# Two attention blocks: packing the output rows and softmax sums of all heads densely by on-chip transfers, with one normalisation and one output projection per batch element

## The chip, the cores and the metric

The kernel runs on one core of a Trainium2 chip. The metric is the device time of one execution, in microseconds. Five engines run their own instruction streams and meet at semaphores: PE (TensorE, matrix products), DVE (VectorE), ACT (ScalarE), POOL (GpSimd) and SP (SyncE), which here issues nearly all transfers. A wait is an instruction in the stream of the engine that waits, so everything behind it on that engine waits too.

## The reference, cut to what matters

The program is a two-layer transformer: attention, mixture of experts, attention again, and two local-attention layers. Only the two attention blocks are touched. For each of 8 batch elements (512 tokens, 128 channels, 16 heads of 8 channels) both compute

```
scores = q[h] @ k[h].T * scale          # 512 x 512 per head
out[h] = softmax(scores) @ v[h]         # 512 x 8 per head
y = concat(out over 16 heads) @ Wo + bo # 128 x 128 projection
x = x + gate * y
```

Block 0 is causal and shares one key/value head among its query heads; block 1 is not causal and has 16 key/value heads.

## The kernel before, in words

`attend` (L608) is called once per block. A batch element is cut into 4 **units** of 4 heads. A unit has 16 **tiles** (`k`, `h`): 128 of the 512 keys for one head. Loops run batch element, unit `q`, `k`, `h`; the first and the last batch element are written out, the 6 between them are a hardware loop. So a block has 8 x 4 = 32 units.

Each unit goes through the scores twice. The first scores (`a_tile`, L703, run two units ahead) give the row maxima (`maxima`, DVE, L920). `split_max` (POOL, L858) splits them into three bf16 parts, `turn_max` (PE, L721) transposes them, `copy_rows` (ACT, L830) copies them to `mrows`, and `move_max` (SP, L667) moves them with 4 small on-chip transfers into rows 72 to 74 of the query tile `Q`, one per head. The second scores (`b_tile`, L733) therefore come out with the maximum already subtracted. Their first tile in a unit waits for these 4 transfers (`m_loaded`). `exp` (ACT, L821) turns each into `probs`; block 0 then masks future keys on POOL (`mask_future`, L875). `pv` (L744) multiplies 4 heads' `probs` with `V`; one head takes 32 partitions of the bank `OB`: 8 with output rows, one with the softmax sum (a column of ones in `vpad`, L196), 23 with zeros.

Normalising a unit, one unit later: `copy_out` (ACT, L835) copies `OB` to `osum`; `turn_sums` (PE, L760, 4 transposes) turns it; `invert_sums` (DVE, L930) inverts the 16 columns of sums; `repeat_inverses` (POOL, L884) repeats each 32 times; `spread_inverses` (PE, L770, 4 transposes) turns that back; `normalise` (DVE, L937) multiplies; `out_project` (PE, L778) adds the unit's part of the projection in bank `YB`, with a `wo` that is padded with zeros. After 4 units `output` (DVE), `residual` (POOL) and `store` (SP) finish the batch element.

The order is written out by hand. PE takes in each tile step first `a_tile`, then `b_tile`. In step (1,3) come `turn_max` and `pv`, `out_project` is at (1,1), `turn_sums` at (2,1), `spread_inverses` at (3,1), and the last `pv` of a unit is at (0,3) of the next. SP's order in a unit is the following: wait until the unit before has ended its last `pv` (L683), 13 loads for the unit three ahead (`load`, L648: 9 to `Q`, 3 to `K`, 1 to `V`), then `move_max` for the next unit, and in unit 2 also one store and one load. The banks are 3 for first scores, 2 for second scores, and `OB`, `MB`, `YB`.

Of the kernel before, what the change touches and what calls it, by code (L numbers as in the profile page):

```python
# [11 lines left out]
ALU = mybir.AluOpType  # L12
# [3 lines left out]
P = 128  # L16
# [3 lines left out]
UNITS = 4  # L20
# [126 lines left out]
def setup_projection(g):  # L147
# [35 lines left out]
    with nc.Block() as block:  # L183
# [7 lines left out]
        def _(pool):  # L191
# [4 lines left out]
            pool.memset(g.vpad[:, :, :, D:D + 1], 1.0)  # L196
# [367 lines left out]
def setup_attention(g):  # L564
# [4 lines left out]
    g.wo = g.sb("wo", [P, 2, UNITS, C])  # L569
# [6 lines left out]
    g.zero = g.sb("zero", [P, CH * UH * VW])  # L576
    g.seen = g.sb("seen", [P, 1])
    g.osum = g.sb("osum", [P, N])
    g.rsum = g.sb("rsum", [P, CH, UH])
    g.rspread = g.sb("rspread", [P, CH, UH, VW])  # L580
# [6 lines left out]
        "m_loaded", "b_scores", "exp", "masked", "pv", "o_copied", "sums", "rsum", "rspread", "spread", "onorm", "yacc",  # L587
# [4 lines left out]
    with nc.Block() as block:  # L592
        @block.sync
        def _(sp):
            sp.dma_start(g.wo[:, :, :, :], g.ins["wo"]).then_inc(g.as_["setup"], 16)
            sp.dma_start(g.bo[:, :], g.ins["bo"]).then_inc(g.as_["setup"], 16)
            sp.wait_ge(g.as_["setup"], 32 * n_setup)
# [10 lines left out]
def attend(g, layer, x, x_out):  # L608
# [36 lines left out]
    with nc.Block() as block:  # L645
        @block.sync
        def _(sp):
# [25 lines left out]

            def store(i):
# [22 lines left out]
            batches(sp, batch)  # L697
            store(hi)
# [3 lines left out]
        def _(pe):  # L702
# [18 lines left out]
            def turn_max(i, u):  # L721
# [3 lines left out]
                if u >= 2:  # L725
                    pe.wait_ge(s["onorm"], i * 4 + u - 2)
# [6 lines left out]
            def b_tile(i, q, k, h):  # L733

                n = q * per + k * UH + h
                t0 = first_query(k)
# [23 lines left out]
            def turn_sums(i, q, m):  # L760

                pe.wait_ge(s["o_copied"], i * 4 + q + 1)
                pe.wait_ge(s["onorm"], i * 4 + q)
                if m is not None:
                    pe.wait_ge(s["mrows"], i * 4 + m + 1)
                for k in range(CH):
                    mm = pe.transpose(MB[:, k * P:(k + 1) * P], g.osum[:, k * P:(k + 1) * P], g.ident[:, :])
                mm.then_inc(s["sums"], 1)

            def spread_inverses(i, q):  # L770

                pe.wait_ge(s["rspread"], i * 4 + q + 1)
# [1446 lines left out]
```

## Time and profile before

| | us |
|---|---|
| median of 3 runs | 2834.71 (2826.03 to 2836.15) |
| the profiled execution's own time | 2839.19 |
| its span | 2837.5 |
| busy PE / DVE / ACT / POOL | 2243.7 / 1628.8 / 1321.0 / 1076.5 |
| granted PE clock, mean | 0.881 of 2.4 GHz |

"Busy" is the time in which an engine has an instruction under way; matmuls overlap, so the busy time of PE is more than its work. The second scores run from 206 to 1623 us, with the expert stage between the two blocks. Times in the rows are microseconds from the start of the span, unless marked ns. SPq is SP's own queue of instructions: the time of such a row is the time that issuing took, not that of the transfer.

### The profile page before, as it was taken

Reading aid. Unit: us, or ns where it says so; the run is one execution under the profiler, and the core shown is the slowest. Engines: PE = TensorE matmul, PEld = TensorE weight load, DVE = VectorE, ACT = ScalarE, POOL = GpSimd, SP = SyncE. Lnnn points to the kernel's source line nnn. Section 1 sums busy time; section 2 is a strip of 40 time slices with the busy share of each in tenths; the row PEclk is TensorE's granted clock in tenths of the full one; section 3 lists DMA queues with packets and bytes.
Section 4 is the critical chain, followed back from the end, with each engine's and each line's share of the span. In section 5 each row is a group of like instructions: output and inputs, shape, how many; then the busy total and the mean of one; then the engine's idle time right before and its main releaser. Section 6 shows DMA issues by size and latency. Waiting matters only on the chain. (4 is left out here: it accounts for less than half of the span.)

```text
span 2837.5 us, 47372 instructions
## 1 busy us (share of the span) xinstructions
PE 2243.7 (79%) x13156; PEld 1254.2 (44%) x13156; DVE 1628.8 (57%) x3408; ACT 1321.0 (47%) x3058; POOL 1076.5 (38%) x1306
## 2 busy tenths in 40 slices
PE   4649999955381663899999866999999999999996
PEld 2324444434261442233333243555555555555553
DVE  3436666624012332777777436777777677777772
ACT  0115566620130111466666604666666666666662
POOL 2314444422305232011111124655655655555550
PEclk9759999975695665799999958999999999999997
DMA  3322222110223223222222121000000000000000
GB/s 96 123 91 57 69 62 67 55 69 18 73 86 105 69 83 91 67 70 68 65 65 73 31 90 43 9 11 11 15 11 11 12 16 16 22 15 15 15 12 11
DMA packets 114411, 140.99 MB, mean 50 GB/s; under 512 B 15888, under 2 KB 77075, under 8 KB 114064
## 3 DMA queue, kind: packets, MB, share of 16 engines
q1 hardware_dynamic: 112272, 135.74, 16.0%
q0 software_dynamic: 2048, 4.16, 0.5%
q8 instruction: 42, 0.69, 0.1%
q14 instruction: 49, 0.40, 0.0%
HBM read 89.81 MB, written 49.28 MB: 49 GB/s over the span
## 5 line engine op out<-in xcount | busy, mean ns | idle before, releaser
L927 DVE TENSOR_REDUCE M_sb<-bank 128x1 f32<-128x512 f32 (+3 forms) x1024 | 557.2, 583 | 304.7 <-PE bank L718 162.9
L827 ACT ACTIVATE probs_sb<-bank 128x512 f32<-128x512 f32 (+3 forms) x1024 | 487.6, 514 | 306.2 <-PE bank L741 301.3
L1780 ACT ACTIVATE l_p_sb<-bank,l_nb_sb,l_inv_sb 128x192 f32<-128x192 f32 x512 | 257.2, 506 | 369.7 <-DVE l_nb_sb L1964 368.2
L715 PE MATMUL bank<-K_sb,Q_sb 72*128 72x512 bf16 (+3 forms) x1024 | 360.6, 358 | 67.5 <-DMA V_sb<-v_dram 64.3
L741 PE MATMUL bank<-Q_sb,K_sb 75*128 75x512 bf16 (+3 forms) x1024 | 349.3, 346 | 12.5 <-ACT probs_sb L827 9.2
L1875 POOL TENSOR_TENSOR l_pn_sb<-l_p_sb,l_rs_sb 128x384 f32<-128x384 f32 x256 | 228.7, 893 | 181.0 <-DVE l_rs_sb L1970 147.8
L1850 POOL TENSOR_TENSOR l_ts_sb<-l_t_sb 128x512 f32<-128x512 f32 x128 | 162.0, 1266 | 283.1 <-DVE l_t_sb L1919 226.8
L1959 DVE TENSOR_REDUCE l_mx_sb<-bank 128x2 f32<-128x384 f32 x256 | 142.0, 555 | 186.4 <-PE bank L1649 183.3
L1647 PE MATMUL bank<-l_kr_sb,l_qr_sb 128*128 128x192 f32 x1024 | 242.0, 338 | 0.0
L755 PE MATMUL bank<-probs_sb,V_sb 128*32 128x512 f32 (+3 forms) x2048 | 236.9, 527 | 0.9 <-POOL probs_sb L881 0.7
L715 PEld LDWEIGHTS bank<-K_sb,Q_sb 72*128 72x128 bf16 x1024 | 101.1, 99 | 295.6 <-DVE M_sb L927 176.0
L1858 POOL TENSOR_TENSOR l_inv_sb<-l_clip_sb,l_minus_half_sb 128x8 f32<-128x8 f32 x128 | 227.7, 1779 | 0.0
L1647 PEld LDWEIGHTS bank<-l_kr_sb,l_qr_sb 128*128 128x128 f32 x1024 | 167.7, 194 | 83.1 <-issue 55.8
L887 POOL TENSOR_TENSOR rspread_sb<-rsum_sb,zero_sb 128x512 f32<-128x512 f32 x64 | 67.0, 1047 | 334.8 <-DVE rsum_sb L933 334.8
L1657 PE MATMUL bank<-ident_sb,l_pn_sb 128*128 128x128 f32 x1024 | 171.0, 290 | 1.7 <-POOL l_pn_sb L1875 1.7
L1670 PEld LDWEIGHTS bank<-l_pt_sb,l_vt_sb 128*64 128x64 f32 x1792 | 95.9, 139 | 169.0 <-issue 112.3
L1670 PE MATMUL bank<-l_pt_sb,l_vt_sb 128*64 128x128 f32 x1792 | 159.0, 294 | 13.8 <-ACT l_pt_sb L1789 11.4
L1789 ACT ACTIVATE l_pt_sb<-bank 128x512 f32<-128x512 f32 x256 | 152.2, 594 | 19.9 <-PE bank L1657 16.3
L1603 PE MATMUL bank<-lw_sb,l_xs_sb 128*128 128x512 f32 x256 | 137.2, 620 | 30.6 <-DMA l_xs_sb<-hx 23.0
L230 PE MATMUL bank<-x_norm_sb,mean_w_sb 128*128 128x512 f32 x64 | 62.0, 1071 | 124.4 <-DMA x_norm_sb<-x 78.2
L741 PEld LDWEIGHTS bank<-Q_sb,K_sb 75*128 75x128 bf16 x1024 | 99.5, 98 | 132.1 <-ACT probs_sb L827 76.0
L245 ACT ACTIVATE sq_sb<-xc_norm_sb 128x512 f32<-128x512 f32 x32 | 20.1, 627 | 266.6 <-DVE xc_norm_sb L238 266.6
(210 smaller groups left out, 4048.0 us busy)
## 6 DMA issues: line engine op xcount, KB each, us to landing
Q_sb<-qk_dram SPq DMA_DIRECT2D x576, 32.0 KB
v_dram<-vpad_sb SPq DMA_DIRECT2D x16, 1024.0 KB, 8.6
V_sb<-v_dram SPq DMA_DIRECT2D x64, 256.0 KB
qk_dram<-parts_sb SPq DMA_DIRECT2D x96, 128.0 KB
K_sb<-qk_dram SPq DMA_DIRECT2D x96, 96.0 KB
x_norm_sb<-x SPq DMA_DIRECT2D x24, 256.0 KB, 2.7
Q_sb<-mrows_sb SPq DMA_DIRECT2D x256, 3.0 KB
x<-xnew_sb SPq DMA_DIRECT2D x16, 256.0 KB, 2.1
```

Of the source, the lines that this page charges most:

```text
L715: mm = pe.matmul(out[:, 0:width], g.Q[0:RK, slot, h, k * P:(k + 1) * P], g.K[0:RK, slot, hk(h), 0:width], start=True, stop=not causal)
L741: pe.matmul(SB[n % 2][:, t0:N], g.K[0:RM, q, hk(h), k * P:(k + 1) * P], g.Q[0:RM, q, h, t0:N], start=True, stop=True).then_inc(s["b_scores ...
L755: mm = pe.matmul(OB[VW * h:VW * (h + 1), t0:N], g.V[:, slot, k, VW * h:VW * (h + 1)], g.probs[:, k, h, t0:N], start=(k == 0), stop=(k == C ...
L827: act.activation(g.probs[:, k, h, t0:N], SB[n % 2][:, t0:N], ACT.Exp, scale=scale)\
L927: dve.reduce_max(g.M[:, u % 2, k, h:h + 1], SA[ring % 3][:, 0:width], AX.X, negate=True)\
L1647: pe.matmul(out, g.qr[:, e, p, t * P:(t + 1) * P], g.kr[:, p, t * P:t * P + WIN], start=True, stop=False, skip_group_check=True)
L1657: mm = pe.transpose(TB[:, j * P:(j + 1) * P], g.pn[:, n % 2, j // 2, (j % 2) * P:(j % 2 + 1) * P], g.ident[:, :])
L1670: mm = pe.matmul(OB[HD * e:HD * (e + 1), p * P:(p + 1) * P], g.vt[:, t - 1 + j, at:at + HD], g.pt[:, n % 2, 2 * e + j, :], start=(j == 1), ...
L1780: last = act.activation(g.pe_[:, n % 2, e, :], S[n % 2][:, WIN * e:WIN * (e + 1)], ACT.Exp, bias=g.lnb[:, n % 4, e:e + 1], scale=g.linv[:, ...
L1850: pool.tensor_tensor(g.lts[:, w, :, :], g.lt1[:, :, :], g.lt2[:, :, :], ALU.add).then_inc(s["tsum"], 1)
L1858: pool.tensor_tensor(g.linv[:, w, a % CH, :], g.lclip[:, w, :], g.minus_half[:, :], ALU.pow)\
L1875: pool.tensor_tensor(g.pn[:, n % 2, :, W:2 * P], g.pe_[:, n % 2, :, :], g.lrs[:, n % 4, :].unsqueeze(2).broadcast_to([P, 2, WIN]), ALU.mult)\
```

## The change: what it does

Three things are changed in `attend`.

Packing. `vpad` gets 8 columns of ones instead of one, so `pv` gives each head's sum 8 times. After `copy_out`, SP issues 8 on-chip transfers per unit (`pack`): for each head, 8 output rows to the dense tile `opack` and 8 sum rows to `spack`. They stand in SP's order between the 13 loads and `move_max`. `copy_out` waits until the previous unit's packs have landed.

One normalisation per batch element. `turn_sums`, `repeat_inverses` and `spread_inverses` are gone. DVE inverts the 128x512 `spack` once, in unit 0 of the next batch element at (3,0); POOL multiplies at k = 3 of that unit; PE projects with an unpadded `wo` at (1,2,2), into `MB`; `output` moves to (1,2,3) and `residual` to k = 3.

Banks. `YB` is gone, the second scores have three banks, and `b_tile` waits for the exponential of three tiles back instead of two.

```diff
-            pool.memset(g.vpad[:, :, :, D:D + 1], 1.0)
+            pool.memset(g.vpad[:, :, :, D:2 * D], 1.0)
...
-    SA, SB, OB, MB, YB = g.bank[0:3], g.bank[3:5], g.bank[5], g.bank[6], g.bank[7]
+    SA, SB, OB, MB = g.bank[0:3], g.bank[3:6], g.bank[6], g.bank[7]
...
+    PACKS = 2 * UH * 16
...
+            def pack(i, u):
+                sp.wait_ge(s["o_copied"], i * 4 + u + 1)
+                if u % UNITS == 0:
+                    sp.wait_ge(s["onorm"], i)
+                for h in range(UH):
+                    r = (u % UNITS * UH + h) * D
+                    sp.dma_start(g.opack[r:r + D, :], g.osum[VW * h:VW * h + D, :]).then_inc(s["packed"], 16)
+                    sp.dma_start(g.spack[r:r + D, :], g.osum[VW * h + D:VW * h + 2 * D, :]).then_inc(s["packed"], 16)
...
                         load(i, q + 3)
+                    if not (first and q == 0):
+                        pack(i, q - 1)
                     u = m_unit(q, first, last)
                     if u is not None:
                         move_max(i, u)
...
             batches(sp, batch)
+            pack(hi, -1)
             store(hi)
...
-                if u >= 2:
-                    pe.wait_ge(s["onorm"], i * 4 + u - 2)
+                if u == 3:
+                    pe.wait_ge(s["ytmp"], i)
...
-                if n >= 2 or not isinstance(i, int) or i:
-                    pe.wait_ge(s["exp"], i * 64 + n - 1)
-                pe.matmul(SB[n % 2][:, t0:N], g.K[0:RM, q, hk(h), k * P:(k + 1) * P],
+                if ring >= 3:
+                    pe.wait_ge(s["exp"], i * 64 + n - 2)
+                elif ring == 0 and (not isinstance(i, int) or i):
+                    pe.wait_ge(s["exp"], i * 64)
+                pe.matmul(SB[ring % 3][:, t0:N], g.K[0:RM, q, hk(h), k * P:(k + 1) * P],
...
-            def turn_sums(i, q, m):
...
-            def spread_inverses(i, q):
...
+            def out_project(i, mrows):
+                pe.wait_ge(s["onorm"], i)
+                pe.wait_ge(s["mrows"], mrows)
+                pe.matmul(MB[:, :], g.wo[:, layer, :], g.onorm[:, :], start=True, stop=True).then_inc(s["yacc"], 1)
...
-                            if (k, h) == (1, 1) and not (first and q < 2):
-                                out_project(i, q - 2)
-                            if (k, h) == (2, 1) and not (first and q == 0):
-                                turn_sums(i, q - 1, m)
-                            if (k, h) == (3, 1) and not (first and q == 0):
-                                spread_inverses(i, q - 1)
+                            if (q, k, h) == (1, 2, 2) and not first:
+                                out_project(i, i * 4 + 3)
...
-                act.wait_ge(s["onorm"], i * 4 + q)
+                act.wait_ge(s["packed"], (i * 4 + q) * PACKS)
...
-            def repeat_inverses(i, q):
...
+            def normalise(i):
+                pool.wait_ge(s["inverse"], i)
+                pool.wait_ge(s["packed"], i * 4 * PACKS)
+                pool.wait_ge(s["yacc"], i - 1)
+                pool.tensor_tensor(g.onorm[:, :], g.opack[:, :], g.inverse[:, :], ALU.mult).then_inc(s["onorm"], 1)
...
+                        if (q, k) == (0, 3) and not first:
+                            normalise(i)
...
+            def invert_sums(i):
+                dve.wait_ge(s["packed"], i * 4 * PACKS)
+                dve.wait_ge(s["onorm"], i - 1)
+                dve.reciprocal(g.inverse[:, :], g.spack[:, :]).then_inc(s["inverse"], 1)
...
+                            if (q, k, h) == (0, 3, 0) and not first:
+                                invert_sums(i)
```

## Rows read from the trace of the kernel before

**Rows 1.** Busy time by engine, granted clock and DMA share, a stretch of block 1.
```profile
1300.00:1350.00 50.00, 46.67 (x267) 16.90 (x266) 37.35 (x63) 32.69 (x62) 8.05 (x17) 1.00 0.25 74
```
**Rows 2.** Timeline of PE in block 1: start, duration, line [idle before <- releaser].
```profile
1300.64 0.38 PE L741 MATMUL bank<-Q_sb,K_sb 75*128 75x512 bf16 x1
1301.83 0.63 PE L767 MATMUL bank<-ident_sb,osum_sb 128*128 128x128 f32 x4 [0.81 <-ACT mrows_sb L833]
1302.30 0.38 PE L715 MATMUL bank<-K_sb,Q_sb 72*128 72x512 bf16 x1
1302.52 0.38 PE L741 MATMUL bank<-Q_sb,K_sb 75*128 75x512 bf16 x1
...
1305.14 0.60 PE L774 MATMUL bank<-ident_sb,rspread_sb 128*128 128x128 f32 x4
1305.58 0.38 PE L715 MATMUL bank<-K_sb,Q_sb 72*128 72x512 bf16 x1
...
1311.53 1.02 PE L783 MATMUL bank<-onorm_sb,wo_sb 128*128 128x512 f32 x2
1312.39 0.38 PE L715 MATMUL bank<-K_sb,Q_sb 72*128 72x512 bf16 x1
```
**Rows 3.** Timeline of SP's queue in block 1, one unit to the next.
```profile
1310.93 1.04 SPq L656 DMA_DIRECT2D Q_sb<-qk_dram  x3
...
1316.35 2.78 SPq L671 DMA_DIRECT2D Q_sb<-mrows_sb  x4
...
1325.47 1.05 SPq L656 DMA_DIRECT2D Q_sb<-qk_dram  x3
```
**Rows 4.** Timeline of PE: first second-score tile of a unit, block 1.
```profile
1322.33 0.38 PE L741 MATMUL bank<-Q_sb,K_sb 75*128 75x512 bf16 x1
```
**Rows 5.** Timeline of SP's queue in block 0, one unit to the next.
```profile
404.20 1.05 SPq L656 DMA_DIRECT2D Q_sb<-qk_dram  x3
...
409.68 2.77 SPq L671 DMA_DIRECT2D Q_sb<-mrows_sb  x4
...
416.29 1.04 SPq L656 DMA_DIRECT2D Q_sb<-qk_dram  x3
```
**Rows 6.** Timeline of PE: first second-score tile of a unit, block 0.
```profile
413.75 0.38 PE L741 MATMUL bank<-Q_sb,K_sb 75*128 75x512 bf16 x1
```
**Rows 7.** Timelines of SP's queue and of PE, last batch element of block 0.
```profile
578.48 2.69 SPq L671 DMA_DIRECT2D Q_sb<-mrows_sb  x4
...
582.30 0.60 PE L741 MATMUL bank<-Q_sb,K_sb 75*128 75x512 bf16 x2 [0.23 <-DMA Q_sb<-mrows_sb]
```
**Rows 8.** Two lines' issues on SP: duration ns min/median/max, first and last start.
```profile
L656 SPq DMA_DIRECT2D Q_sb<-qk_dram x576: 272/277/1177, 180.1 to 1576.2; - x192
...
L671 SPq DMA_DIRECT2D Q_sb<-mrows_sb x256: 639/640/816, 197.5 to 1608.6; - x128
```
**Rows 9.** Instructions of three lines by source: duration ns min/median/max.
```profile
L1970 DVE RECIPROCAL l_rs_sb<-l_sm_sb x256: 151/157/161, 1739.2 to 2791.0; 128x2 f32<-128x2 f32 x128
L130 DVE RECIPROCAL sil_sb<-sil_sb x1: 253/253/253, 8.9 to 8.9; 128x16 f32<-128x16 f32 x1
L897 POOL TENSOR_TENSOR xnew_sb<-ytmp_sb,xres_sb x16: 1259/1262/1262, 273.3 to 1631.1; 128x512 f32<-128x512 f32 x16
```
**Rows 10.** Timeline of PE in the projection stage of block 0.
```profile
86.02 2.07 PE L230 MATMUL bank<-x_norm_sb,mean_w_sb 128*128 128x512 f32 x2 [4.82 <-DMA x_norm_sb<-in_xT]
```
**Rows 11.** PE's busy time and granted clock in that stage, by windows of 1 us.
```profile
82.00:83.00 1.00, 0.00 (x0) 0.50 0.26 88
...
91.00:92.00 1.00, 1.00 (x5) 0.50 0.25 58
92.00:93.00 1.00, 1.00 (x6) 0.91 0.28 86
```
**Rows 12.** Timeline of PE at the start of block 1, clock 0.50.
```profile
1161.11 0.61 PE L715 MATMUL bank<-K_sb,Q_sb 72*128 72x512 bf16 x1
...
1168.05 1.94 PE L755 MATMUL bank<-probs_sb,V_sb 128*32 128x512 f32 x8
1169.92 0.61 PE L715 MATMUL bank<-K_sb,Q_sb 72*128 72x512 bf16 x1
```

More of the change, by code:

```diff
@@ L575, in setup_attention @@
     g.probs = g.sb("probs", [P, CH, UH, N])
-    g.zero = g.sb("zero", [P, CH * UH * VW])
+    g.zero = g.sb("zero", [P, CH * UH])
     g.seen = g.sb("seen", [P, 1])
     g.osum = g.sb("osum", [P, N])
-    g.rsum = g.sb("rsum", [P, CH, UH])
-    g.rspread = g.sb("rspread", [P, CH, UH, VW])
+    g.opack = g.sb("opack", [P, N])
+    g.spack = g.sb("spack", [P, N])
+    g.inverse = g.sb("inverse", [P, N])
     g.onorm = g.sb("onorm", [P, N])
@@ L586, in setup_attention @@
         "setup", "ones_set", "zero_set", "a_scores", "a_max", "max_turned", "mpart1", "mres", "mpart2", "mpart3", "mrows",
-        "m_loaded", "b_scores", "exp", "masked", "pv", "o_copied", "sums", "rsum", "rspread", "spread", "onorm", "yacc",
+        "m_loaded", "b_scores", "exp", "masked", "pv", "o_copied", "packed", "inverse", "onorm", "yacc",
         "x_loaded", "ytmp", "xnew", "x_stored")}
@@ L735, in b_tile @@
                 n = q * per + k * UH + h
+                ring = n % (UNITS * per)
                 t0 = first_query(k)
@@ L758, in pv @@
                 mm.then_inc(s["pv"], 1)
-            def turn_sums(i, q, m):
[L762 to L768, printed above, removed]
-            def spread_inverses(i, q):
-                pe.wait_ge(s["rspread"], i * 4 + q + 1)
-                for k in range(CH):
-                    mm = pe.transpose(MB[:, k * P:(k + 1) * P], g.rspread[:, k, :, :].rearrange("p h w -> p (h w)"),
-                                      g.ident[:, :])
-                mm.then_inc(s["spread"], 1)
-            def out_project(i, q):
-                w = q % UNITS
-                pe.wait_ge(s["onorm"], i * 4 + q + 1)
-                if w == 0:
-                    pe.wait_ge(s["ytmp"], i)
-                pe.matmul(YB[:, :], g.wo[:, layer, w, :], g.onorm[:, :], start=(w == 0), stop=(w == UNITS - 1),
-                          skip_group_check=True).then_inc(s["yacc"], 1)
+            def out_project(i, mrows):
+                pe.wait_ge(s["onorm"], i)
+                pe.wait_ge(s["mrows"], mrows)
+                pe.matmul(MB[:, :], g.wo[:, layer, :], g.onorm[:, :], start=True, stop=True).then_inc(s["yacc"], 1)
             def batch(i, first, last):
@@ L822, in exp @@
                 n = q * per + k * UH + h
+                ring = n % (UNITS * per)
                 t0 = first_query(k)
@@ L904, in batch @@
                     for k in range(CH):
-                        if k == 2 and not (first and q == 0):
-                            repeat_inverses(i, q - 1)
+                        if (q, k) == (0, 3) and not first:
+                            normalise(i)
                         if causal:
                             mask_future(i, q, k)
-                        if (q, k) == (1, 1) and not first:
+                        if (q, k) == (1, 3) and not first:
                             residual(i)
@@ L914, in _ @@
             batches(pool, batch)
-            repeat_inverses(hi, -1)
+            normalise(hi)
             residual(hi)
@@ L956, in batch @@
                                 maxima(i, u, k, h)
-                            if (k, h) == (1, 2) and q == 1 and not first:
+                            if (q, k, h) == (1, 2, 3) and not first:
                                 output(i)
-                            if (k, h) == (2, 2) and not (first and q == 0):
-                                invert_sums(i, q - 1)
-                            if (k, h) == (3, 3) and not (first and q == 0):
-                                normalise(i, q - 1)
+                            if (q, k, h) == (0, 3, 0) and not first:
+                                invert_sums(i)
             for u in range(2):
@@ L968, in _ @@
             batches(dve, batch)
-            invert_sums(hi, -1)
-            normalise(hi, -1)
+            invert_sums(hi)
             output(hi)
```

37 lines of the change are left out of this document (7 added, 30 removed).

## The prediction, made before the changed kernel was run

> **What bounds the kernel now.** I read the busy times of a stretch of each block first. In block 1 PE is busy 46.67 of 50 us at full clock, DVE 37.35, ACT 32.69 [rows 1]; the rest is PE's. Next I read PE's timeline in order. First and second scores follow each other every 0.22 us (1302.30, 1302.52), and three things break that pace [rows 2]. The transposes of the sums cost 1.44 us (next slot 1300.86, resumed 1302.30, of it 0.81 waiting for ACT), the transposes of the inverses 0.44 us (1305.14 to 1305.58), the projection 0.86 us (1311.53 to 1312.39). That is 2.74 us a unit, and it is what the change removes.
>
> So I asked what would be late next, and read SP's own queue, which the busy table does not list. One unit's circle runs so. SP wakes when the last `pv` of the unit before has ended, issues 13 loads, then 4 moves of the maxima; these land; the second scores of the next unit start; its step (0,3) ends that next last `pv`; SP wakes. In block 1 [rows 3, 4, 7]: from the wake to the end of the moves 8.20 us (1310.93 to 1316.35 + 2.78); landing 1.13 us (issue ended at 578.48 + 2.69 = 581.17, PE released at 582.30, the one clear wait for it); from the first second-score tile to SP's wake 3.14 us (1322.33 to 1325.47). Sum 12.47 us, while the units follow each other every 14.54 us: 2.07 us of slack. In block 0 [rows 5 to 7]: 8.25 + 1.13 + 2.54 (413.75 to 416.29) = 11.92 us of a period of 12.09: slack 0.17 us. The reader is to see that in block 0 the circle through SP already sets the pace almost alone, and that in block 1 PE does, with the circle 2 us behind it.
>
> **What the change puts into that circle.** `pack` stands in SP's order between the 13 loads and `move_max`. All 8 issues thus come before the moves that the next unit's second scores wait for. Its own wait (`o_copied`) costs nothing: the copy of one bank stands six exponentials into the unit, and the loads take 5.4 us to issue (1310.93 to 1316.35 [rows 3]). The trace has no transfer of 8 rows from on-chip memory to on-chip memory. The two nearest are the move of the maxima, also from on-chip to on-chip, at 0.640 us of issue (2.78 for 4, thus 0.693 each with the gap), and the load of 8 rows of `Q` at 0.277 [rows 8], 0.33 with the same gap. The first has the same source, destination and queue but 3 rows; the second the same rows but its source is off-chip. I take 0.693, because what is common (source and destination) looks to me the likelier cause than 3 rows instead of 8, and keep 0.33 as the low end. 8 x 0.693 = 5.54 us a unit.
>
> Block 1: 12.47 + 5.54 = 18.01 us against 14.54. Block 0: 11.92 + 5.54 = 17.46 against 12.09. So the removed PE work becomes idle time: PE would need 14.54 - 2.74 + 0.86 / 4 = 12.0 us a unit in block 1 and, with less to do, still less in block 0. It would stand before the first second-score tile for about 6 us a unit, waiting for the moves.
>
> **The clock.** A pause as long as that has a second price. In the projection stage PE paused 4.82 us before 86.02; the granted clock was 0.50 from within the pause until 92, six microseconds after the restart [rows 10, 11]. The 3.14 us between the first second-score tile and SP's wake lie in the circle, and at 0.50 (1.2 instead of 2.4 GHz) they are longer. At the start of block 1, at clock 0.50, 16 score matmuls took 6.94 us (1161.11 to 1168.05), 0.434 each against 0.22, and a `pv` 1.87 us [rows 12]. Eight matmuls thus cost 1.7 us more and the `pv` about 0.9: some 2.5 us. For block 0, where the first-score tiles at k = 0 and that `pv` have 128 columns instead of 512, I take 1.5 (bounds 0 and 2.5). A unit then takes 20.5 us in block 1 and 19.0 in block 0, that is +6.0 and +6.9.
>
> How many units: 3 of the first batch element, 24 of the loop, 1 of the last: 28 a block. 28 x (6.0 + 6.9) = 361 us.
>
> **The smaller terms.** The inverse: 2 columns took 157 ns and 16 took 253 [rows 9], 6.9 ns a column, so 512 take about 3.7 us (bounds: 0.6 us, a 128x512 maximum on DVE [rows 1], and 3.7). It comes once per batch element, in DVE's queue at (3,0) of unit 0, and behind it wait three maxima of 0.6 us each (37.35 / 63 [rows 1]) and through them the first scores of the next unit. The packs land 5.42 + 5.54 + 1.13 = 12.1 us after SP's wake, the inverse ends at 15.8, the maximum that PE's next tile needs at 16.4, the fourth tile is written at 18.2. With 0.9 for the pair and 1.9 for the `pv` at the low clock this is 0.7 us later than the circle, at full clock 1.9. I take 1 us, 14 times: 14. `normalise` on POOL (like the residual's 1.26 us [rows 9]) follows it, and in block 0 the mask stands behind it; it ends near 17.1, before the `pv` that needs the mask. The last batch element has no loads after unit 0; in units 1 and 2 the packs (5.54) stand where the loads (5.42) were, but begin only after the copy: +4 each (bounds 0 and 6), 16 for both blocks. At the end of a block, issue, landing, inverse and multiplication (5.5 + 1.1 + 3.7 + 1.3) replace the transposes (0.47 + 0.44), a repetition and one projection with their waits: +7, 14 for both. The third bank removes short waits of PE for ACT, which lie inside the new pause: 0 (were PE the bound, 0.2 a unit). The smaller `wo`, the wider column of ones and the transferred 128 KB a unit cost nothing: the transfer engines are busy a quarter of the time [rows 1].
>
> **Sum.** 361 + 14 + 16 + 14 = 405 us on the profiled execution's 2839.2: 3244. That execution was 4.5 us above the median of the runs, so I predict 3240.
>
> **A rule against this.** The Trainium skill, DMA: Bandwidth & Descriptors, "Anatomy of one DMA", gives the sequencer's dispatch of a transfer as about 50 ns, and "Issuing engines are not separate DMA queues" calls the time of issuing "usually small relative to the DMA itself". By that the packs would add 8 x 0.05 = 0.4 us to the circle, the units would take about 12.3 and 12.9 us, and the kernel would come to some 2800. The trace does not agree: the shortest issue of all `Q` loads took 272 ns [rows 8].
>
> **The rivals.**
> - *The packs issue like the `Q` loads.* 8 x 0.33 = 2.64: circles of 14.56 and 15.11, +2.5 and +0.6 us, 28 x 3.1 = 87; with the low clock up to 4.0 us more per pair of units, 199. With 14 x 1.9 for the inverse and the ends, 2965 to 3080, middle 3015. For it: 8 rows. Against it: the source. Chance 0.20.
> - *The clock stays up.* 28 x (5.37 + 3.47) = 248, + 27 (inverse) + 8 + 14: 3130. For it: between the pauses PE works without a break for some 12 us [rows 2], and in 1300 to 1350 the clock is 1.00 [rows 1]. Against it: rows 10 and 11. Chance 0.17.
> - *The circle does not close, because issuing the packs costs next to nothing: faster.* Then PE's freed 2.74 us count until the old circle (12.47 and 11.92) sets the pace: -2.07 and -0.17 us, 28 x -2.24 = -63, with the ends about 2790. It decides at 16 x = 2.24, an issue of 0.14 us each. No issue in rows 8 is below 0.27. Chance 0.04, of which 0.01 within 0.5% of before.
> - *Dearer than forecast*: issues above 0.7 us, or a landing held up behind the loads. 1 us a unit is 60 us: 3300 and more. Chance 0.08.
>
> **How the numbers follow.** The forecast (move-like issue, low clock) has 0.51 and its own range 3180 to 3310. The range that reaches to the others is 3000 to 3320: it takes in the warm case and the upper two thirds of the cheap one. About 0.5% is what can be told from no change here. Every case but the third is slower by more: slower 0.96, faster 0.03, same 0.01.
>
> **What the profile would show.** SP's queue: 8 more issues a unit between the load of `V` and the moves, 0.64 us each (right) or 0.3 (first rival). PE at line 741's successor: idle time that ends with the transfer from `mrows`, about 5 to 6 us a unit, some 300 us in all, where rows 7 show 0.23 us and such waits are rare. The granted clock in both blocks: 0.7 to 0.85 in place of 1.00; at 1.00 the second rival holds. One reciprocal of 3 to 4 us per batch element. Units 19.0 us apart in block 0 and 20.5 in block 1. If PE waits mostly for DVE or ACT, or the units come under 12.5 us in block 1, my reading is wrong.

## The result and the profile after

The changed kernel takes 3192.94 us (median of 4 runs, 3192.41 to 3195.09) against 2833.44 us (2826.03 to 2836.15) for the kernel before on the same chip. The ratio is 1.127, with a 95% interval of 1.1247 to 1.1293. Forecast were 3240 us, that is +405; measured are +359.5. The span of the profiled execution grew from 2837.5 to 3193.1 us, and the mean granted clock fell from 0.881 to 0.798.

The page of the changed kernel's profile gives the busy times and, per group of instructions, the busy time and the mean ns of one, then the idle time just before it with what ended most of it:

```profile
PE 2346.5 (73%) x12548; PEld 1230.4 (39%) x12548; DVE 1641.2 (51%) x3296; ACT 1321.7 (41%) x3058; POOL 1031.2 (32%) x1258
...
L759 PE MATMUL bank<-Q_sb,K_sb 75*128 75x512 bf16 (+3 forms) x1024 | 445.2, 440 | 191.1 <-DMA Q_sb<-mrows_sb 188.0
L730 PE MATMUL bank<-K_sb,Q_sb 72*128 72x512 bf16 (+3 forms) x1024 | 431.1, 427 | 160.9 <-DVE M_sb L916 95.6
```

The second scores (L759) now wait 188.0 us for the transfer of the maxima; before, such a wait was 0.23 us where one was to be seen at all [rows 7]. The first scores (L730) wait 95.6 us for DVE's maxima, which stand behind the large reciprocal. By the view of waits the first is a pause of 4.2 us on the mean, 45 times, the second one of 4.6 us, 21 times.

SP's queue in block 1, one unit to the next, in place of [rows 3]:

```profile
1519.26 1.06 SPq L658 DMA_DIRECT2D Q_sb<-qk_dram  x3
...
1524.19 0.41 SPq L666 DMA_DIRECT2D V_sb<-v_dram  x1
1524.77 0.71 SPq L683 DMA_DIRECT2D opack_sb<-osum_sb  x1
1525.53 0.64 SPq L684 DMA_DIRECT2D spack_sb<-osum_sb  x1
...
1529.54 0.62 SPq L684 DMA_DIRECT2D spack_sb<-osum_sb  x1
1530.29 2.78 SPq L673 DMA_DIRECT2D Q_sb<-mrows_sb  x4
...
1539.42 1.05 SPq L658 DMA_DIRECT2D Q_sb<-qk_dram  x3
```

Each pack starts 0.66 to 0.68 us after the one before it (the second 0.76), and together the eight fill 5.52 us (1524.77 to 1530.29) between the load of `V` and the moves. PE in the same unit, in place of [rows 4] (start, duration, line, idle before):

```profile
1529.60 0.39 PE L730 MATMUL bank<-K_sb,Q_sb 72*128 72x512 bf16 x1
1534.17 0.61 PE L759 MATMUL bank<-Q_sb,K_sb 75*128 75x512 bf16 x1 [4.18 <-DMA Q_sb<-mrows_sb]
1534.57 0.63 PE L730 MATMUL bank<-K_sb,Q_sb 72*128 72x512 bf16 x1
...
1537.27 1.94 PE L773 MATMUL bank<-probs_sb,V_sb 128*32 128x512 f32 x8
```

PE stops at 1529.99, waits for the moves, and starts again at 1534.17. The view by windows of 1 us (length of the window, PE's busy time, granted clock, DMA share, GB/s) shows what that pause does, as [rows 11] did in the projection stage:

```profile
1530.00:1531.00 1.00, 0.00 (x0) 1.00 0.18 31
...
1532.00:1533.00 1.00, 0.00 (x0) 0.74 0.01 3
1533.00:1534.00 1.00, 0.00 (x0) 0.50 0.02 6
...
1538.00:1539.00 1.00, 1.00 (x8) 0.50 0.00 0
1539.00:1540.00 1.00, 1.00 (x8) 0.85 0.00 0
```

The clock falls from 1.00 to 0.50 inside the pause and is at 0.50 (1.2 GHz) until after 1539. The score matmuls then follow each other every 0.425 us instead of every 0.22, and the eight of the `pv` take 1.94 us instead of 1.06.

**Where the 355.6 us of the span are.** The last store of block 0 stands at 790.03 us, before at 600.57: +189.5. The last store of block 1 stands at 1983.45, before at 1632.35: another +161.6. The remaining 4.5 lie behind. Inside the blocks the unit, read from one load of `V` to the next (line 666, before 664), took in us, in the steady batch elements of the loop:

| | before | after, most units | after, unit behind the inverse | four units, mean before and after |
|---|---|---|---|---|
| block 0 | 12.0 to 12.6 | 18.1 to 18.4 | 19.86 | 48.8 and 74.4 |
| block 1 | 14.3 to 14.7 | 20.1 to 20.3 | 22.0 | 58.2 and 82.2 |

Four units of the loop were shorter, one of block 0 (17.1) and three of block 1 (18.8 to 19.2). In each of them the pause before the second scores was only 1.3 to 1.7 us, and PE went on at full clock.

### The profile page after: what moved, and what is told of

Its sections match the earlier page's. It is cut to its first block and busy times, and to the rows that moved or that the text cites. A ratio compares the mean times of both kernels' runs of the same rounds, so it can differ in the third digit from the quotient of the medians.

```text
span 3193.1 us, 46324 instructions
## 1 busy us (share of the span) xinstructions
PE 2346.5 (73%) x12548; PEld 1230.4 (39%) x12548; DVE 1641.2 (51%) x3296; ACT 1321.7 (41%) x3058; POOL 1031.2 (32%) x1258
## 5 line engine op out<-in xcount | busy, mean ns | idle before, releaser
L818 ACT ACTIVATE probs_sb<-bank 128x512 f32<-128x512 f32 (+3 forms) x1024 | 495.4, 516 | 654.3 <-PE bank L759 641.5
L759 PE MATMUL bank<-Q_sb,K_sb 75*128 75x512 bf16 (+3 forms) x1024 | 445.2, 440 | 191.1 <-DMA Q_sb<-mrows_sb 188.0
L730 PE MATMUL bank<-K_sb,Q_sb 72*128 72x512 bf16 (+3 forms) x1024 | 431.1, 427 | 160.9 <-DVE M_sb L916 95.6
L773 PE MATMUL bank<-probs_sb,V_sb 128*32 128x512 f32 (+3 forms) x2048 | 307.7, 670 | 4.3 <-ACT osum_sb L829 1.9
L730 PEld LDWEIGHTS bank<-K_sb,Q_sb 72*128 72x128 bf16 x1024 | 116.9, 114 | 482.6 <-DVE M_sb L916 229.6
L759 PEld LDWEIGHTS bank<-Q_sb,K_sb 75*128 75x128 bf16 x1024 | 120.2, 119 | 322.0 <-DMA Q_sb<-mrows_sb 200.8
L871 POOL TENSOR_TENSOR seen_sb<-zero_sb 128x1 f32<-128x1 f32 x128 | 24.7, 193 | 361.9 <-ACT probs_sb L818 357.0
L733 PE MATMUL bank<-mask_sb,identb_sb 128*128 128x128 bf16 x512 | 139.5, 273 | 0.0
```

Source lines behind the costliest of these rows:

```text
L730: mm = pe.matmul(out[:, 0:width], g.Q[0:RK, slot, h, k * P:(k + 1) * P], g.K[0:RK, slot, hk(h), 0:width], start=True, stop=not causal)
L759: pe.matmul(SB[ring % 3][:, t0:N], g.K[0:RM, q, hk(h), k * P:(k + 1) * P], g.Q[0:RM, q, h, t0:N], start=True, stop=True).then_inc(s["b_sco ...
L773: mm = pe.matmul(OB[VW * h:VW * (h + 1), t0:N], g.V[:, slot, k, VW * h:VW * (h + 1)], g.probs[:, k, h, t0:N], start=(k == 0), stop=(k == C ...
L818: act.activation(g.probs[:, k, h, t0:N], SB[ring % 3][:, t0:N], ACT.Exp, scale=scale)\
```

## The experiments

Two theories stood against each other at first. *The circle*: SP's issue of the packs lies ahead of the moves that PE waits for, and PE's pause costs clock as well. *The extra work*: it is the large inverse, the landing of the packs or the packed data that costs, wherever they stand. All ratios below are to the kernel before, run on the same chip beside the experiment.

**The packs alone, in the kernel before.** The kernel before keeps its own transposes, and the eight packs are issued into two buffers that nothing reads:

```diff
+                    if not (first and q == 0):
+                        pack(i, q - 1)
                     u = m_unit(q, first, last)
                     if u is not None:
                         move_max(i, u)
```

> The kernel before, unchanged in its arithmetic, with the 8 packs of each unit added at the same place in SP's order (behind the 13 loads, before the 4 moves); nothing reads what they write. Theory (the packs' issue in the circle, and the low clock in the pause behind it, are nearly the whole loss; the PE work that the change removed only turned into pause): units of 17.8 to 20.2 us in block 1 and 17.3 to 18.1 in block 0, none of the 14 longer units behind the inverse: 3160 us (3120 to 3195), so no slower than the changed kernel although PE keeps all its old work. Rival A (the removed PE work did bring something): slower than the changed kernel, 3193 + 56 x up to 2.7 = up to 3340. Rival B (the loss is in the new order of DVE and POOL): 2835 to 2870.

Measured: 3156.74 us (3155.56 to 3158.99), ratio 1.116 [1.1139, 1.1181]. So the circle's price is there without the inverse, without the new normalise and with all of PE's old work: 327 of the 360 us. Its unit took 17.9 to 18.4 us in block 0 and 20.0 on the mean in block 1 with the transposes and the projection of every unit, which the changed kernel no longer has. PE's removed work was worth nothing; it had become part of the pause. PE waits for the moves 58 times, 159.3 us in all and 4.5 at most, against 45 times and 188.0 in the changed kernel:

```profile
PE bank L756 <- DMA Q_sb<-mrows_sb: 159.3, 58, 4.5
```

**The dose.** Only the rows are packed, the sums are not, four issues instead of eight. The tile of sums is set to ones once, so this kernel leaves out the division by the sums:

```diff
                     sp.dma_start(g.opack[r:r + D, :], g.osum[VW * h:VW * h + D, :]).then_inc(s["packed"], 16)
-                    sp.dma_start(g.spack[r:r + D, :], g.osum[VW * h + D:VW * h + 2 * D, :]).then_inc(s["packed"], 16)
```

> The changed kernel without the 4 packs of the sums of each unit (their tile is set to ones once, so nothing is divided by the sums); the 4 packs of output rows remain. Theory (issue time in the circle, 0.667 us each): 4 x 0.667 = 2.67 us off each of some 56 units, 150 us, and up to 40 more where the shorter pause keeps the clock up: 3040 us (3000 to 3055). Rival A (bytes or landing): half of 64 KB a unit less, under 10 us. Rival B (the waits around the inverse dominate): under 30 us.

Measured: 3001.52 us (2998.70 to 3006.23), ratio 1.0602 [1.0575, 1.0630]: 191 us less than the changed kernel for half of the packs. Four units took 63.0 us in block 0 and 67.7 in block 1 (before 48.8 and 58.2, changed 74.4 and 82.2). The four missing issues are 5.52 / 2 = 2.76 us a unit, 155 in 56 units; the other 36 us I put down to the clock, which no run separates here. PE's timeline of this kernel has pauses after which the matmuls run at full pace, and others after which they do not:

```profile
1512.72 0.39 PE L730 MATMUL bank<-K_sb,Q_sb 72*128 72x512 bf16 x1
1515.61 0.39 PE L759 MATMUL bank<-Q_sb,K_sb 75*128 75x512 bf16 x1 [2.50 <-DMA Q_sb<-mrows_sb]
...
1566.16 0.61 PE L759 MATMUL bank<-Q_sb,K_sb 75*128 75x512 bf16 x1 [2.25 <-DMA Q_sb<-mrows_sb]
...
1636.06 0.39 PE L759 MATMUL bank<-Q_sb,K_sb 75*128 75x512 bf16 x1 [2.98 <-DMA Q_sb<-mrows_sb]
```

After the pauses of 2.50 and 2.98 us PE went on at 0.22 us a matmul, after that of 2.25 us at 0.425. So between 2 and 3 us the length of the pause alone does not tell what follows; the rows do not show what else decides. The units of this kernel ran now at the one pace, now at the other (14.9 to 17.4 us in block 1, that behind the inverse left out).

**The order.** All eight packs stay, but SP issues them behind the moves:

```diff
-                    if not (first and q == 0):
-                        pack(i, q - 1)
                     u = m_unit(q, first, last)
                     if u is not None:
                         move_max(i, u)
+                    if not (first and q == 0):
+                        pack(i, q - 1)
```

> The changed kernel with one edit: in SP's order the 8 packs of a unit stand behind the 4 moves of the maxima instead of before them. Same transfers, same PE, DVE and POOL work. Theory (the packs cost because their issue stands in the circle from the last pv through SP to the next unit's second scores): the circle loses the packs, and what remains is SP's own sum of issues, 5.4 + 2.8 + 5.3 us and the store, about 13.8 us a unit in both blocks instead of 20.2 and 18.1. The packs of a batch element's last unit then land some 14.7 us after SP's wake, so the inverse and the unit behind it come about 8 us late, 14 times. Sum about 3000 us (2960 to 3050). Rival A (the transfers cost by their traffic or landing, wherever they are issued): 3150 to 3200, as the changed kernel. Rival B (the new order of PE, DVE and POOL costs, not SP): 3190.

Measured: 3061.91 us (3053.49 to 3073.11), ratio 1.0820 [1.0780, 1.0861]. The order alone gives back 131 us, so the same transfers of the same bytes cost less where PE doesn't wait behind them. It is 62 us more than I had expected. The expectation had a pace of 13.8 us and 8 us once per batch element, and in the trace both come out larger. SP now has no rest at all; the next loads wait for the packs' issue:

```profile
1515.22 1.05 SPq L658 DMA_DIRECT2D Q_sb<-qk_dram  x3
...
1520.65 2.83 SPq L673 DMA_DIRECT2D Q_sb<-mrows_sb  x4
1523.66 0.68 SPq L683 DMA_DIRECT2D opack_sb<-osum_sb  x1
...
1529.30 1.05 SPq L658 DMA_DIRECT2D Q_sb<-qk_dram  x3
```

The 25 issues of a unit take 14.08 us in a row (1515.22 to 1529.30), and the units between two inverses took 14.1 to 16.3 us in block 1. And the packs of a batch element's last unit land later, while DVE's queue stands at the inverse that wants them. DVE, then PE behind it:

```profile
1574.28 3.35 DVE L922 RECIPROCAL inverse_sb<-spack_sb 128x512 f32<-128x512 f32 x1 [8.98 <-DMA spack_sb<-osum_sb]
```
```profile
1578.24 0.61 PE L730 MATMUL bank<-K_sb,Q_sb 72*128 72x512 bf16 x1 [11.14 <-DVE M_sb L916]
```

That unit took 24.8 us in block 1 and 23.1 in block 0, some 10 and 8 more than its neighbours; a pause of 11 us once per batch element came in the place of the four small ones.

**The inverse.** Only 16 of its 512 columns are computed; this kernel leaves the others at one:

```diff
-                dve.reciprocal(g.inverse[:, :], g.spack[:, :])
+                dve.reciprocal(g.inverse[:, 0:16], g.spack[:, 0:16])
```

> The changed kernel with the inverse taken of 16 of the 512 columns (the others stay at a constant), so it lasts about 0.25 us instead of 3.35; its place and its wait for the packs are kept. Theory (the inverse lies on the path only where it ends behind the moves, 1.4 us a batch element, and once in full at the end of each block): 14 x 1.4 + 2 x 3.1 = 26 us gained, 3167 us (3155 to 3180). Rival (the inverse is a main cost: 3.35 us and the maxima behind it on every batch element): 14 x 3.1 + more, 3130 or less.

Measured: 3170.59 us (3165.74 to 3174.92), ratio 1.1196 [1.1167, 1.1226], 22 us less than the changed kernel. The unit behind the inverse takes 18.3 us in block 0 and 19.5 to 20.2 in block 1, as its neighbours do. So the inverse costs 1.6 to 1.8 us a batch element and not its length of 3.35: the rest lay in the pause. It is more at the end of a block, where PE's wait for the normalised rows falls from 12.10 to 9.01 us. The two together, 14 x 1.7 + 2 x 3.1 = 30 us, are more than the 22 measured; two of the units that took 18.8 to 19.2 us in the changed kernel took 20.2 here.

**The clock.** 24 matmuls into a bank that is overwritten anyway stand before the wait for the moves, in three units of each four. They keep PE at work in the pause:

```diff
                 if k + h == 0:
+                    if filled:
+                        for _ in range(24):
+                            pe.matmul(SB[ring % 3][:, 0:N], g.K[0:RK, q, 0, 0:P], g.Q[0:RK, q, 0, 0:N],
+                                      start=True, stop=True)
                     pe.wait_ge(s["m_loaded"], (i * 4 + q + 1) * 16 * UH)
```

> The changed kernel with 24 extra matmuls (bf16, 512 columns, some 5.3 us at full clock, results overwritten by the unit's first second-score tile) put into PE's pause before it waits for the moves of the maxima; in 42 of the units, not in those behind the inverse, where PE waits for DVE first. Theory (the pause lowers the clock, and the low clock stretches the part of the circle between restart and SP's wake by 2.1 us in block 1 and 0.8 in block 0): granted clock near 1.00 in these units, 21 x 2.1 + 21 x 0.8 = 61 us gained, 3130 us (3110 to 3160). Rival (the low clock is a bystander, only the issue time counts): 3193, or slower if the extra work runs past the moves' landing.

Measured: 3187.19 us (3170.17 to 3196.14), ratio 1.1264 [1.1225, 1.1303], which can't be told from the changed kernel's. The trace shows why the sum failed and the mechanism did not. PE and then SP:

```profile
1522.59 5.34 PE L760 MATMUL bank<-Q_sb,K_sb 72*128 72x512 bf16 x24
1527.77 0.38 PE L763 MATMUL bank<-Q_sb,K_sb 75*128 75x512 bf16 x1
```
```profile
1522.25 2.78 SPq L673 DMA_DIRECT2D Q_sb<-mrows_sb  x4
1530.67 1.05 SPq L658 DMA_DIRECT2D Q_sb<-qk_dram  x3
```

The clock was 1.00 from 1523 to 1531, and from the first second-score tile to SP's wake it took 2.90 us (1527.77 to 1530.67) where the changed kernel took 5.25 (1534.17 to 1539.42). Filled units took 17.8 to 17.9 us instead of 20.15 in block 1 and mostly 16.8 to 17.2 instead of 18.1 in block 0. But in the unit shown the fillers ran 1.6 us past the landing (1522.25 + 2.78 + 1.13 = 1526.2, against 1527.77), and the filled unit behind the one with the inverse took 19.4 to 21.4 us in block 1 and 18.4 to 20.8 in block 0. One filled unit of block 0 took 26.3 us. There PE was still at 0.50 when it came to the fillers, and they took twice their time:

```profile
484.26 10.45 PE L760 MATMUL bank<-Q_sb,K_sb 72*128 72x512 bf16 x24
```

PE had no pause in the windows from 475 to 495 us and stayed at 0.50 all the same, so full work in the pause did not bring the clock back there.

In the next kernel I filled only before units 0 and 3, behind which the fillers should not run past the landing:

```diff
-                            b_tile(i, q, k, h, q != 1 and not (first and q == 0) and not (last and q))
+                            b_tile(i, q, k, h, q in (0, 3) and not (first and q == 0) and not (last and q))
```

> The changed kernel with the 24 extra matmuls in PE's pause only ahead of units 0 and 3, that is not behind the inverse and not in the unit after it, where in the first such run they ended 1.6 us after the moves had landed. Theory (the low clock behind the pause costs 2.3 us in a unit of block 1 and 1.2 in one of block 0): 15 units a block, 15 x 3.5 = 52 us faster than the changed kernel, 3140 us (3125 to 3165). Rival (the clock is a bystander): 3193.

Measured: 3175.45 us (3164.45 to 3186.15), ratio 1.1207 [1.1171, 1.1244]: 18 us less than the changed kernel, a third of what I had expected. The filled units were short again (in block 1 one of the two always 17.9 us and the other 17.8, or 19.5 to 19.8 in three cases; in block 0 mostly 16.8 to 17.3), and four units took 79.2 and 72.4 us instead of 82.2 and 74.4. One unit of 26.1 us in block 0, and 6 us between the blocks, took some of it back in the profiled execution. The unit is the same case as above: its fillers took 10.45 us from 683.07. PE was busy throughout from 670 to 700 us and the granted clock was 0.50; the last third of it (length, busy time of PE, PEld, DVE, ACT, POOL, clock, DMA share, GB/s):

```profile
690.00:700.00 10.00, 10.00 (x47) 4.51 (x49) 2.58 (x7) 4.65 (x9) 0.97 (x4) 0.50 0.07 19
```

The cause of the 6 us stays open.

**Is the old circle's start the bound of the kernel before?** Its loads begin when PE has come to the end of the unit's second scores instead of its last `pv`; only `V` waits for that:

```diff
-                            sp.wait_ge(s["pv"], i * 16 + 4 * q)
-                        load(i, q + 3)
+                            sp.wait_ge(s["b_scores"], i * 64 + 16 * q)
+                            load(i, q + 3, i * 16 + 4 * q)
```

> The kernel before with one edit in SP's order: the 12 loads of Q and K wait only until the unit before has ended its second scores, and the load of V alone waits for its last pv; so the loads leave the circle. Theory (before, PE's own work sets the pace in block 1, and in block 0 PE and the circle are within 0.2 us): nothing, 2815 to 2835. Rival (the circle is what bounds the kernel before): block 0 down by 1 us a unit or more, 2800 or less.

Measured: 2830.16 us (2821.96 to 2836.70), ratio 0.9997 [0.9982, 1.0012]. In block 0 four units took 48.6 us against 48.8, in block 1 58.2 as before. So in neither block did the circle set the pace of the kernel before, also not in block 0, where the prediction had it do so almost alone with 0.17 us of slack. More slack in the circle was worth nothing where PE has as much work as before.

**One transfer a unit, off-chip and back.** To see what the removed PE work is worth with a short circle, the bank with the unit's rows and sums is stored whole (one issue a unit, behind the moves) and fetched dense (two issues a batch element); the inverse is taken in four pieces of 128 columns, the projection one unit later:

```diff
+                sp.dma_start(g.o_dram.rearrange("b u p n -> (b u) p n")[i * 4 + u], g.osum[:, :]).then_inc(s["kept"], 16)
...
+                sp.dma_start(g.opack[:, :], src[:, 0:D, :]).then_inc(s["packed"], 16)
+                sp.dma_start(g.spack[:, :], src[:, D:2 * D, :]).then_inc(s["packed"], 16)
```

> As the run with off-chip rows, but with the loads where the kernel before has them. Theory (the circle without packs, 12.47 us in block 1 and 11.92 in block 0, sets the pace instead of PE's 12.0): 28 x (2.05 + 0.15) = 62 us faster than before, less some 7 for the quarters of the inverse: 2775 us (2755 to 2800), about 40 us slower than the same kernel with early loads. Rival (PE work is what counts): no difference between the two.

Measured: 2874.28 us (2866.35 to 2881.15), ratio 1.0169 [1.0146, 1.0191]: 319 us less than the changed kernel, and still slower than before; I had forecast faster. Three units of a batch element took 12.25 to 12.45 us each in block 1, where the old circle's sum was 12.47 and PE's work 12.0, and PE waits for the moves a moment:

```profile
1430.14 0.39 PE L765 MATMUL bank<-Q_sb,K_sb 75*128 75x512 bf16 x1 [0.28 <-DMA Q_sb<-mrows_sb]
```

The fourth took 17.4 to 22.0. DVE had been sent to the inverse before the sums were back, and stood in front of the maxima:

```profile
1436.64 0.95 DVE L929 RECIPROCAL inverse_sb<-spack_sb 128x128 f32<-128x128 f32 x1 [2.75 <-DMA spack_sb<-o_dram]
```

**The same with early loads.**

> The idea of the change without its 8 packs: each unit's rows are stored off-chip by one transfer behind the moves, and two transfers per batch element fetch all output rows and all sums densely; inverse in four quarters in unit 1, projection and output in unit 2; and the 12 loads of Q and K start as in the run of the kernel before with early loads. Theory (with nothing dear in the circle and the loads out of it, PE's own work sets the pace: 14.54 - 2.74 + 0.22 = 12.0 us a unit in block 1, some 11 in block 0): 28 x (2.4 + 1.1) = 98 us faster than before, 2735 us (2700 to 2770). Rival (off-chip latency or DVE's quarters take the place): 2780 to 2850.

Measured: 2818.67 us (2810.69 to 2828.75), ratio 0.9959 [0.9936, 0.9982]. Four units took 54.6 us in block 1, 3.6 below before, and 48.7 in block 0, the same as before. In the kernel before the early loads gave nothing, here 56 us: with the work on PE gone, the circle decides. DVE stands for the fetched sums here too (2.66 and 2.59 us in the two such rows of block 1 from 1330 to 1400). But that wait is not the whole of the 84 us by which the expectation of 2735 was missed: the last experiment below takes it away and is only 16 us faster.

**The pieces spread over units 1 to 3, fetch in unit 1**, without and with early loads:

> The same without the early loads: the circle through SP is that of the kernel before, without packs. Theory: its units in the run with off-chip rows were 12.25 us in block 1 and 12.3 to 12.6 in block 0 wherever the inverse did not disturb, against 14.54 and 12.1 before; so 28 x 2.25 - 28 x 0.3 = 55 us faster than before, 2775 us (2760 to 2795), and some 60 us slower than the same kernel with early loads. Rival (PE's work is the bound, the circle plays no part): the two differ by less than 10 us.

> The run with off-chip rows and early loads, with two shifts: the two fetches come in unit 1 instead of unit 0, and the four quarters of the inverse are spread over units 1 to 3, with multiplication, projection and output in unit 3. Theory (in the run before this one DVE stood in the queue for the fetched sums, 2.6 to 3.6 us per batch element, and four quarters in one unit pushed it over PE's pace, which also lowered the clock behind it; its other units already ran at 10.2 us in block 0): units of about 12.1 us in block 1 and 10.3 in block 0 throughout, 28 x (2.4 + 1.8) = 118 us faster than before: 2710 us (2695 to 2735). Rival (something else than the place of the inverse held those units): 2790 or more.

Measured: 2920.38 us (2913.15 to 2926.04), ratio 1.0310 [1.0281, 1.0338], and 2902.43 us (2889.04 to 2909.40), ratio 1.0248 [1.0221, 1.0275]. Both were missed by my own placing: the fetch was issued after DVE had come to the first piece, at 1426.51 - 5.53 = 1420.98 in the first of the two kernels:

```profile
1422.74 0.59 SPq L687 DMA_DIRECT2D spack_sb<-o_dram  x1
```
```profile
1426.51 0.95 DVE L927 RECIPROCAL inverse_sb<-spack_sb 128x128 f32<-128x128 f32 x1 [5.53 <-DMA spack_sb<-o_dram]
```

Once per batch element a unit of 21 us came out in block 1 of that kernel; the other three took 12.3 to 14.4. A piece of 0.95 us that waits in DVE's queue thus cost the whole pipeline some 8 us.

**The fetch one unit earlier**, with early loads:

```diff
-                    if q == 1 and not first:
+                    if q == 0 and not first:
                         gather(i)
```

> The run with the spread inverse and early loads, with the two fetches issued at the end of unit 0 again instead of unit 1. In the run before it they were issued about 1 us after DVE had come to its first quarter (unit 1, step (3,2)) and DVE stood 5.3 us for them, PE 6.2 us behind it. With the fetches in unit 0 the sums landed 4 us into unit 1 in the first off-chip run, and DVE comes to that step some 6.5 us after the one at which it waited then. Theory (only the place of the fetch held those units; elsewhere PE's own work sets the pace, 12.1 us in block 1 and 10.3 in block 0): DVE waits for no fetch, 28 x (2.4 + 1.8) = 118 us faster than before: 2715 us (2695 to 2745). Rival (the spread inverse or the later projection holds the units by itself): 2790 or more.

Measured: 2802.29 us (2797.24 to 2815.93), ratio 0.9908 [0.9884, 0.9933], 0.9% faster than the kernel before by the median of the runs, 12.2% faster than the changed one. Of DVE's 16 waits for the fetch only the two at the ends of the blocks are left in the view of waits. Of block 1 four units took 50.3 us instead of 58.2, with PE at full clock. Busy time of PE, PEld, DVE, ACT, POOL, then clock and DMA share, with one window of block 0 beside it:

```profile
250.00:550.00 300.00, 262.11 (x1977) 121.53 (x1975) 187.79 (x405) 166.38 (x424) 107.06 (x291) 0.84 0.31 91
...
1200.00:1550.00 350.00, 340.00 (x1919) 101.65 (x1917) 301.96 (x480) 259.12 (x507) 40.37 (x124) 1.00 0.38 108
```

In block 0 four units took 51.4 us, 2.6 more than before, and there the forecast of 2715 broke. SP, then PE of a stretch of it:

```profile
401.15 0.36 SPq L694 DMA_DIRECT2D x<-xnew_sb  x1
...
402.73 1.08 SPq L659 DMA_DIRECT2D Q_sb<-qk_dram  x3
...
407.76 0.40 SPq L669 DMA_DIRECT2D V_sb<-v_dram  x1
408.30 2.77 SPq L676 DMA_DIRECT2D Q_sb<-mrows_sb  x4
...
413.56 0.66 SPq L688 DMA_DIRECT2D opack_sb<-o_dram  x1
```
```profile
410.77 0.23 PE L740 MATMUL bank<-K_sb,Q_sb 72*128 72x128 bf16 x1 [2.19 <-DMA V_sb<-v_dram]
...
412.26 0.61 PE L767 MATMUL bank<-Q_sb,K_sb 75*128 75x512 bf16 x1 [1.20 <-DMA Q_sb<-mrows_sb]
```

Both waits of PE stand before the fetch (413.56), so it isn't the fetch that causes them. SP issues nothing from 397.86 to 401.15: it waits for the finished rows of the batch element before, in order to store them (L694), and the unit's loads (from 402.73) and moves (408.30) stand behind that. After the two waits PE's matmuls took 0.61 to 0.63 us again, the clock of 0.50; over 250 to 550 us it was 0.84. PE also waits 1.5 us for DVE's maxima in the unit after, where the first piece of the inverse stands (426.71). That these waits are the whole loss of block 0 was read, not tried.

## Why the prediction was right, and where its sizes were off

**The circle through SP was right, and it is shown.** From SP's wake to the end of the moves it took 13.81 us (1519.26 to 1533.07), predicted 8.20 + 5.54 = 13.74; the landing took 1.10 (1533.07 to 1534.17), predicted 1.13. The packs took 5.52 us of it, predicted 5.54. The move-like bound was the right end: a pack issues in 0.625 us, a move in 0.641, so between these two the number of rows, 8 or 3, made no difference to speak of:

```profile
L683 SPq DMA_DIRECT2D opack_sb<-osum_sb x256: 624/625/732, 222.8 to 1971.8; - x128
```

The packs alone put +327 us on the kernel before; behind the moves they cost 131 us less. The figure weighed against the change, about 50 ns of dispatch (the Trainium skill, DMA: Bandwidth & Descriptors, "Anatomy of one DMA"), would have made it some 2800 us. By that section's heading it is for transfers issued by GpSimd; these are issued by SyncE, so it was no rule for this case, and SyncE's issue of 0.625 us decides.

One statement beside it was wrong: in block 0 of the kernel before the circle did not set the pace almost alone. With the loads out of it nothing changed.

**The low clock was right in kind, a little smaller in size.** The stretch from the first second-score tile to SP's wake came to 5.25 us in block 1, where the sum had 3.14 + 2.5 = 5.64. In block 0 it came to 3.31, where the sum had 2.54 + 1.5 = 4.04. With the pause filled the same stretch took 2.90 and 2.04 us at full clock. Block 0, the changed kernel, then the filled one, PE and SP:

```profile
399.67 0.61 PE L759 MATMUL bank<-Q_sb,K_sb 75*128 75x512 bf16 x1 [5.66 <-DMA Q_sb<-mrows_sb]
402.98 1.05 SPq L658 DMA_DIRECT2D Q_sb<-qk_dram  x3
```
```profile
412.49 0.38 PE L763 MATMUL bank<-Q_sb,K_sb 75*128 75x512 bf16 x1
414.53 1.06 SPq L658 DMA_DIRECT2D Q_sb<-qk_dram  x3
```

So between the two clocks lie 5.25 - 2.90 = 2.35 us a unit in block 1 and 3.31 - 2.04 = 1.3 in block 0, near the 2.5 and 1.5 of the sum.

**The term that was mis-sized.** The sum set the clock's price on top of the stretch as it was in the kernel before. That stretch holds short waits of PE for ACT, 0.24 us in block 1 (3.14 - 2.90) and 0.5 in block 0 (2.54 - 2.04). One of them is this:

```profile
414.82 0.39 PE L741 MATMUL bank<-Q_sb,K_sb 75*128 75x512 bf16 x1 [0.24 <-ACT probs_sb L827]
```

At 0.50 they are gone, and not because of the third bank. The kernel before with idle packs has two banks, and the same stretch took 5.26 us in block 1 (1496.83 to 1502.09) and 3.35 in block 0:

```profile
414.57 0.60 PE L756 MATMUL bank<-Q_sb,K_sb 75*128 75x512 bf16 x1 [3.12 <-DMA Q_sb<-mrows_sb]
417.92 1.07 SPq L659 DMA_DIRECT2D Q_sb<-qk_dram  x3
```

So the third bank was worth nothing here, as predicted. Against the kernel before the low clock cost 2.35 - 0.24 = 2.1 us a unit in block 1 and 1.3 - 0.5 = 0.8 in block 0, where the sum had 2.5 and 1.5: 28 x (0.4 + 0.7) = 31 us, of which 21 are the waits for ACT. The mean clock, forecast at 0.7 to 0.85 in both blocks, was 0.67 from 250 to 550 us, a little below that, and 0.78 from 1450 to 1900, by the view by windows.

**PE's removed work was worth nothing here, as predicted.** The kernel before with idle packs, which keeps that work, has the same units of 18 and 20 us; it is 36 us *faster* than the changed kernel. The difference is about what the inverse and the ends cost, 14 x 1.7 + 2 x 8.6 = 41 us.

**The smaller terms.** The inverse took 3.35 us for 512 columns (predicted 3.7). It made its unit 1.6 to 1.8 us longer instead of 1; taking it away, at the ends too, gave 22 us, where 14 stood in the sum without the ends. The ends: the last `pv` ended at 1967.1 and the store began 16.4 us later, before 7.8 us (1624.6 to 1632.35), +8.6 for a predicted 7. The largest part of the 16.4 is a wait of 12.10 us for the normalised rows, which the timeline of PE shows; DVE's inverse stands in it:

```profile
1964.85 2.21 PE L773 MATMUL bank<-probs_sb,V_sb 128*32 128x512 f32 x16
1979.16 2.08 PE L781 MATMUL bank<-onorm_sb,wo_sb 128*128 128x512 f32 x2 [12.10 <-POOL onorm_sb L879]
```
```profile
1974.41 3.35 DVE L922 RECIPROCAL inverse_sb<-spack_sb 128x512 f32<-128x512 f32 x1 [35.12 <-DMA spack_sb<-osum_sb]
```

**The sum.** Predicted 28 x 6.9 = 193 and 28 x 6.0 = 168 for the units, 44 for the rest. Measured from store to store, 189.5 and 161.6 for the blocks with all in them, 351.1 where 405 had stood. In steady batch elements four units grew by 25.6 and 24.0 us, predicted 28.6 and 25. Those are 7 x (3.0 + 1.0) = 28 of the 54 us that are missing, with the longer unit behind the inverse already in it. The rest is in the first and last batch elements, whose units I counted like the loop's, with 16 us more for the last: the first units of block 1 behind the ramp grew by 4.8, 3.9 and 4.3 us (18.98, 18.53, 20.39 against 14.22, 14.68, 16.1), not by 6. I had expected PE to wait for the moves some 300 us; it was 188.0, and 95.6 more for DVE in the units behind the inverse, 284 together.

**The rivals.** Packs as cheap as the loads of `Q`: no, 0.625 us. The clock stays up: no, it is 0.50 in the restart of nearly every steady unit; it stays up in the four short ones named above, and with fewer packs in more. Faster because the circle doesn't close: no for this kernel. The last experiment, which has no pack ahead of its moves and starts its loads early, is faster than before, by 0.9%.

## What to carry to other kernels

Before moving work from a busy engine to transfers, lay out the queue that must issue them as a circle, from the event that wakes it to the event that it enables, and add each issue at the price of a transfer with the same source and destination. Behind the transfer that the busy engine waits for, one store of 0.39 us a unit left three units of four at 12.25 to 12.45 us, while eight packs there filled the queue and set a pace of 14.1 us and more. Ahead of it an issue costs in full, and where it makes a pause of some 4 us, a price in clock comes on top (2.1 us a unit in block 1). Where a queue of another engine holds the work of the next steps, put an operation that waits for a transfer there only when the transfer has long landed.

## What the runs showed of the hardware

- A transfer from on-chip to on-chip memory took 0.625 us of SP's time with 8 rows of 2 KB and 0.640 with 3 rows of 1 KB, the store of 128 rows to off-chip memory 0.39, and the dense fetch of 128 rows back 0.59 to 0.66. No run kept one of these shapes and changed only its source.
- The reciprocal took 3.353 us for 512 columns and 0.95 for 128, that is 6.3 ns for each further column, against 6.9 between the 2 and the 16 columns of [rows 9].
- PE paused 4.18 us and went on at 0.50 for 5 us. In the kernel with half of the packs it went on at full clock after pauses of 2.50 and 2.98 us, and at 0.50 after one of 2.25 us.
- In the kernel filled before units 0 and 3, PE was busy for all of 670 to 700 us and its granted clock was 0.50 in all of it; a restart at 0.50 did not always end after 5 us.
